# Edge attention of a graph network: both blocks of a pair in one operation, products written slot-innermost, one sum a pair

## The chip, the cores and the metric

One core of a Trainium2 chip (trn2). The metric is device time in microseconds (us) of one execution, lower is better. Engines: TensorE (PE), VectorE (DVE), ScalarE (ACT), GpSimd (POOL), SyncE (SP).

## What is computed

Two layers over 12500 nodes with 32 features and 200000 edges sorted by target. The first is a spline convolution (five gather and scatter stages that the change leaves alone). The second, which the change touches, is attention over each node's incoming edges with 4 heads, then a gated update:

```python
feat = (h @ W_gat).reshape(N, H, F)
e = leaky_relu(el[src] + er[dst], 0.2)
emax = segment_max(e, dst)
ee = exp(e - emax[dst])
alpha = ee / segment_sum(ee, dst)[dst]
agg = segment_sum(feat[src] * alpha[:, :, None], dst)
gi = agg.reshape(N, H * F) @ W_ih.T + b_ih
gh = h @ W_hh.T + b_hh
r, z = sigmoid(i_r + h_r), sigmoid(i_z + h_z)
n = tanh(i_n + r * h_n)
out = x + elu((1 - z) * n + z * h)
```

Since the sum over edges is linear, the kernel sums weight times `h[src]` (32 numbers a head, 4 x 32 = 128 a node) and applies `W_gat` and `W_ih` afterwards as one matrix.

## The kernel before

The change lies in `attention_flow` alone, the last stage. Nodes lie 128 to a block (one a partition), 98 blocks, worked in 49 pairs. Each node's edges are contiguous rows of the table `rows4` in HBM, 36 numbers an edge (32 features and 4 scores); one pass takes up to 40 edges of every node (RUN = 40), and here one pass is enough.

**POOL** (L1605 to L1660) runs two things in turn. `gather_turn` issues 32 indirect gathers (L1614), each of which fetches 128 rows of 36 numbers from the node table into a ring of four slots; SP writes a full slot out to `rows4` (L1586) and loads the next indices (L1564). `load_runs` (L1618) waits for those writes, then until both products of the pair before are made (`prod_made`, L1624), since `run` has one buffer a block of the pair, then issues two indirect loads (L1629), one for each block, of 40 x 36 numbers a partition. After a lead of two turns, every pair of blocks has its turn of gathers ahead of its run load until the gathers are through: there are 32 gathers between the run loads of pairs 0 to 46, and none behind that of pair 46.

**VectorE** (L1786 to L1812) does for each pair: `scale` of the pair before (L1695: divide the sums by the denominators), `attend` (L1790: copy of the next start rows for POOL at L1793, then `body` for block 0 and for block 1), and `gate` of the pair before (L1712). `body` (L1734) is a chain in which each step waits for the one ahead: mask of missing edges (L1742), score (L1744, L1746), leaky relu (L1748), maximum over edges (L1750, L1752), differences (L1754, L1756), the new maximum to `top` (L1758), the sum of the weights (L1760) once ScalarE has made the exponential (L1820), the denominator (L1766, L1771), the old sum times its factor as a 41st product (L1767), four products of 10 edges each (L1774), and their sum (L1783). The products of one block are 41 x 4 x 32, the edge ("slot") outermost, so that the sum over slots reads elements 128 words apart:

```python
dve.tensor_reduce(sums[:, v, :], prod[:, v, :, :, :].rearrange("p s h f -> p (h f) s"), X, ALU.add)
```

**ScalarE** (L1814 to L1854) makes the exponentials (`weigh`), copies for TensorE (`lift`), the sigmoid, tanh and exponential of the gates (`open_gates`), and copies each block's sums into the accumulator (`take`, L1822), which `scale` waits for (`added`, L1697). **TensorE** (L1856) transposes and multiplies for the gates.

Nothing orders the engines but these semaphores: each engine's instructions run in the order written. Outside the attention stage the text uses only the durations of single lines: L139 and L298 (sums over contiguous elements), L207 (a dense cast), L213 (a copy to every eighth word) and L761 (an operation with two inputs whose elements lie five words apart in all operands).

Of the kernel before, what the change touches and what calls it, by code (L numbers as in the profile page):

```python
# [29 lines left out]
FEAT = 32  # L30
HID = 64
K = 125
HEADS = 4
BIG = 1e30
# [6 lines left out]
SLOPE = 0.2  # L41
# [3 lines left out]
GW = FEAT + HEADS  # L45
RUN = 40
# [13 lines left out]
def bc(ap, shape):  # L60
    return ap.to_broadcast(shape)
# [1448 lines left out]
def attention_flow(nc, c, d, sem, out):  # L1510
# [6 lines left out]
    prod_made, summed, added = (sem(f"at_{x}") for x in ("prod_made", "summed", "added"))  # L1517
# [7 lines left out]
    steps, gate_steps = 13, 7  # L1525
    H3 = 3 * FEAT
    HALF = NB // 2
    full = (N // P) * P
    with nc.Block() as block, ExitStack() as ctx:
        sb, ps, _ = allocators(nc, ctx)  # L1530
# [8 lines left out]
        out_of = sb("at_out_of", [P, 2, RUN])  # L1539
        score = sb("at_score", [P, 2, RUN, HEADS])  # L1540
        peak, total = sb("at_peak", [P, 2, HEADS]), sb("at_total", [P, 2, HEADS])
        weight = sb("at_weight", [P, 2, RUN + 1, HEADS])
        prod = sb("at_prod", [P, 2, RUN + 1, HEADS, FEAT])
        sums = sb("at_sums", [P, 2, P])
# [118 lines left out]
        def _(dve):  # L1663
# [10 lines left out]
            dve.sem_inc(summed, 2)  # L1674
# [20 lines left out]
            def scale(i, item):  # L1695
                pair = bass.ds(i * 2, 2)
                dve.wait_ge(added, item * 2 + (NB + 2))  # L1697
                dve.wait_ge(turned, item + 1)
                dve.tensor_copy(hs[:, :, :], c.h[:, pair, :]).then_inc(gate_seq, 1)
                dve.tensor_scalar(rden[:, :, :], c.acc[:, pair, P:P + HEADS], 1e-30, None, ALU.max).then_inc(gate_seq, 1)  # L1700
                dve.wait_ge(gate_seq, item * gate_steps + 2)
                dve.reciprocal(rden[:, :, :], rden[:, :, :]).then_inc(gate_seq, 1)
                dve.wait_ge(gate_seq, item * gate_steps + 3)
                for v in range(2):
                    last = dve.tensor_tensor(xs[:, v, :, :],
                                             c.acc[:, bass.ds(i * 2 + v, 1), 0:P].rearrange("p b (h f) -> p (b h) f", h=HEADS),
                                             bc(rden[:, v, :].unsqueeze(2), [P, HEADS, FEAT]), ALU.mult)
                    if v == 0:
                        last.then_inc(gate_seq, 1)
                last.then_inc(scaled, 1)  # L1710

            def gate(i, item):  # L1712
# [4 lines left out]
                dve.wait_ge(gate_seq, item * gate_steps + 5)  # L1717
                dve.tensor_tensor(cand[:, :, :], g_ps[:, :, 2 * FEAT:H3], gap[:, :, :], ALU.add).then_inc(shaped, 1)
                dve.wait_ge(curved, item + 1)
                dve.tensor_tensor(gap[:, :, :], c.h[:, pair, :], cand[:, :, :], ALU.subtract).then_inc(gate_seq, 1)  # L1720
                dve.wait_ge(gate_seq, item * gate_steps + 6)
                dve.tensor_tensor(gap[:, :, :], gap[:, :, :], rz[:, :, FEAT:2 * FEAT], ALU.mult).then_inc(gate_seq, 1)
                dve.wait_ge(gate_seq, item * gate_steps + 7)
# [10 lines left out]
            def body(b, item, v):  # L1734
                def after_step(k):
                    dve.wait_ge(seq, item * steps + k)  # L1736

                el = run[:, v, :, FEAT:GW]
                er = bc(c.elr[:, bass.ds(b, 1), HEADS:2 * HEADS], [P, RUN, HEADS])
                best = top[:, bass.ds(b, 1), :].rearrange("p b h -> p (b h)")  # L1740
                s = score[:, v, :, :]
                dve.tensor_scalar(out_of[:, v, :], slots[:, :], left[:, bass.ds(b, 1)], -BIG, ALU.is_ge, ALU.mult)\  # L1742
                    .then_inc(seq, 1)
                dve.tensor_tensor(s, el, er, ALU.add).then_inc(seq, 1)  # L1744
                after_step(2)
                dve.tensor_tensor(s, s, bc(out_of[:, v, :].unsqueeze(2), [P, RUN, HEADS]), ALU.add).then_inc(seq, 1)  # L1746
                after_step(3)
                dve.scalar_tensor_tensor(s, s, SLOPE, s, ALU.mult, ALU.max).then_inc(seq, 1)  # L1748
                after_step(4)
                dve.tensor_reduce(peak[:, v, :], s.rearrange("p s h -> p h s"), X, ALU.max).then_inc(seq, 1)  # L1750
                after_step(5)
                dve.tensor_tensor(peak[:, v, :], peak[:, v, :], best, ALU.max).then_inc(seq, 1)  # L1752
                after_step(6)
                dve.tensor_tensor(weight[:, v, 0:RUN, :], s, bc(peak[:, v, :].unsqueeze(1), [P, RUN, HEADS]),  # L1754
                                  ALU.subtract).then_inc(exp_ready, 1)
                dve.tensor_tensor(weight[:, v, RUN, :], best, peak[:, v, :], ALU.subtract).then_inc(exp_ready, 1)  # L1756
                dve.wait_ge(exp_ready, item * 2 + 2)  # L1757
                dve.tensor_tensor(best, peak[:, v, :], peak[:, v, :], ALU.max).then_inc(seq, 1)  # L1758
                dve.wait_ge(exp_done, item + 1)  # L1759
                dve.tensor_reduce(total[:, v, :], weight[:, v, 0:RUN, :].rearrange("p s h -> p h s"), X, ALU.add)\  # L1760
                    .then_inc(seq, 1)

                dve.wait_ge(summed, item + 1)
                dve.wait_ge(added, item + 1)  # L1764
                den = c.acc[:, bass.ds(b, 1), P:P + HEADS].rearrange("p b h -> p (b h)")
                dve.tensor_tensor(den, den, weight[:, v, RUN, :], ALU.mult).then_inc(seq, 1)  # L1766
                dve.tensor_tensor(prod[:, v, RUN, :, :],  # L1767
                                  c.acc[:, bass.ds(b, 1), 0:P].rearrange("p b (h f) -> p (b h) f", h=HEADS),
                                  bc(weight[:, v, RUN, :].unsqueeze(2), [P, HEADS, FEAT]), ALU.mult)
# [12 lines left out]
                dve.wait_ge(added, item + (NB - 1))  # L1782
                dve.tensor_reduce(sums[:, v, :], prod[:, v, :, :, :].rearrange("p s h f -> p (h f) s"), X, ALU.add)\  # L1783
                    .then_inc(summed, 1)

            n = dve.value_load(c.run_passes[0:1, 0:1], min_val=1, max_val=EP // RUN + 1)  # L1786
            with dve.Fori(0, n) as o:
                dve.wait_ge(pass_begun, o + 1)
                dve.sem_inc(dve_turn, 1)
                def attend(i):  # L1790
                    for v in range(2):
                        dve.wait_ge(run_loaded[v], i * 16 + 16)  # L1792
                    dve.tensor_copy(run_at[:, :], runs[:, bass.ds(i * 2 + 2, 2)]).then_inc(run_at_made, 1)  # L1793
                    for v in range(2):
                        body(i * 2 + v, o * NB + i * 2 + v, v)
# [3 lines left out]
                attend(0)  # L1799
                with dve.Fori(1, HALF) as i:  # L1800
                    scale(i - 1, o * HALF + i - 1)
                    attend(i)
                    gate(i - 1, o * HALF + i - 1)
# [11 lines left out]
        def _(act):  # L1815
            act.sem_inc(added, NB)
# [24 lines left out]
            with act.Fori(0, n) as o:  # L1841
                for v in range(2):
                    weigh(o * NB + v, v)
                for v in range(2):
                    take(v, o * NB + v, v)
                with act.Fori(1, HALF) as i:
                    lift(o * HALF + i - 1)
                    for v in range(2):
                        weigh(o * NB + i * 2 + v, v)
                    open_gates(o * HALF + i - 1)  # L1850
                    for v in range(2):
                        take(i * 2 + v, o * NB + i * 2 + v, v)
                lift(o * HALF + HALF - 1)
                open_gates(o * HALF + HALF - 1)  # L1854
# [137 lines left out]
```

## Time and profile before

| | |
|---|---|
| median of 3 runs | 11170.6 us (11164.8 to 11173.6) |
| profiled execution, its span from first to last instruction | 12528.6 us |
| the profiled execution's own time, beside its span | none is given but the span |
| attention stage in it | about 9790 us to the end |
| VectorE busy | 62% |
| POOL busy | 60% |
| TensorE busy | 52% |
| ScalarE busy | 23% |

The profiled execution is longer than the timed ones by 1358 us. Register and branch instructions aren't counted as busy. The busy shares are means over stages with different limits, and a row of one stage has to be read against the time of that stage.

### The profile page before, as it was taken

The numbers are of one execution on the slowest core, as the hardware profiler recorded it, in microseconds if no ns is written. First come the engines' busy times: TensorE is split into PE (matmuls) and PEld (weight loads), VectorE is DVE, ScalarE is ACT, GpSimd is POOL, SyncE is SP. The second block draws the span as 40 slices with busy tenths as digits, with TensorE's granted clock in tenths as the row PEclk, the third lists the DMA queues.
The fourth block names the chain that finished last, engine by engine and source line by source line (L and its number), as shares of the span: only waits on it lengthen the run. The fifth ranks groups of instructions, "written<-read, shape, count | busy, mean of one in ns | idle before, by whom it ended". The sixth has DMA issues, their size and how long they took to land. (4 is left out here: it accounts for less than half of the span.)

```text
span 12528.6 us, 178083 instructions
## 1 busy us (share of the span) xinstructions
PE 6505.4 (52%) x38968; PEld 5397.9 (43%) x38968; DVE 7716.2 (62%) x17239; ACT 2933.1 (23%) x8407; POOL 7476.5 (60%) x7456
## 2 busy tenths in 40 slices
PE   3466666666475799999994444545555100000000
PEld 2355555555475677777764434434454100000000
DVE  9844444444498676666664444544576267777777
ACT  0011111111132344344432222322343000000001
POOL 5155555655200888888886888888800566666663
PEclk9966666666698999999997667766777555555555
DMA  1210000000733444444443333333322212221221
GB/s 41 65 36 2 2 2 2 2 2 2 14 41 50 93 93 94 92 94 95 92 93 49 50 51 53 54 50 52 54 42 34 35 49 50 51 50 48 51 54 40
DMA packets 1788557, 605.09 MB, mean 48 GB/s; under 512 B 1595943, under 2 KB 1729575, under 8 KB 1788260
## 3 DMA queue, kind: packets, MB, share of 16 engines
q1 hardware_dynamic: 1078132, 311.05, 12.8%
q0 software_dynamic: 255648, 274.30, 10.7%
q10 hardware_dynamic: 454736, 19.28, 3.0%
q8 instruction: 15, 0.25, 0.0%
q14 instruction: 26, 0.21, 0.0%
HBM read 430.75 MB, written 172.95 MB: 48 GB/s over the span
## 5 line engine op out<-in xcount | busy, mean ns | idle before, releaser
L1222 PE MATMUL c_acc<-c_spread_sb,c_basis_sb 128*125 128x256 f32 (+1 forms) x12544 | 2599.2, 376 | 1502.8 <-issue 655.0
L1222 PEld LDWEIGHTS c_acc<-c_spread_sb,c_basis_sb 128*125 128x125 f32 x12544 | 2266.5, 231 | 1803.5 <-issue 1536.3
L1614 POOL DMA_INDIRECT at_ring<-gat_table,at_place x1568 | 1585.7, 1011 | 1188.5 <-issue 1188.5
L609 POOL DMA_INDIRECT rec<-rk_rec,rk_place x1568 | 1619.3, 1033 | 1110.1 <-DVE rk_place L497 620.7
L1321 ACT ACTIVATE c_sums<-c_acc 125x512 f32<-125x512 f32 (+1 forms) x3136 | 1489.3, 490 | 2258.7 <-PE c_acc L1222 1298.6
L961 POOL DMA_INDIRECT c_ring<-hid_table,c_at x1568 | 1707.1, 1089 | 478.9 <-issue 443.2
L961 POOL DMA_INDIRECT c_ring<-feat_table,c_at x1568 | 1602.7, 1022 | 478.1 <-issue 462.9
L1084 DVE TENSOR_TENSOR c_spread_sb<-c_mark,c_rin 128x512 f32<-128x512 f32 (+1 forms) x3136 | 1745.2, 557 | 60.3
L1871 PE MATMUL gr_hps<-ident,gr_hs 128*32 128x128 f32 x98 | 29.8, 408 | 2473.7 <-issue 2066.3
L492 DVE CUSTOM_DVE_ANT_0 rk_junk_l<-rk_look_ps,rk_hi 128x98 bf16<-128x98 f32 x1568 | 402.2, 257 | 1324.1 <-remote 821.1
L1234 PE MATMUL c_mix<-c_sums,c_w 125*64 125x256 f32 (+1 forms) x9408 | 1037.3, 401 | 187.6 <-issue 133.8
L554 PE MATMUL rk_look_ps<-rk_table,rk_lo_t 128*128 128x98 f32 x3136 | 908.7, 425 | 379.5 <-DVE rk_before L492 327.4
L1871 PEld LDWEIGHTS gr_hps<-ident,gr_hs 128*32 128x32 f32 x98 | 6.4, 109 | 2488.1 <-issue 2078.1
L554 PEld LDWEIGHTS rk_look_ps<-rk_table,rk_lo_t 128*128 128x128 f32 x3136 | 705.4, 292 | 503.3 <-DVE rk_before L492 404.2
L1783 DVE TENSOR_REDUCE at_sums<-at_prod 128x128 f32<-128x5248 f32 x98 | 873.3, 8911 | 24.0 <-issue 14.1
L1234 PEld LDWEIGHTS c_mix<-c_sums,c_w 125*64 125x64 f32 (+1 forms) x9408 | 627.4, 132 | 559.2 <-issue 304.0
L530 PE MATMUL rk_rows_ps<-ident,rk_cols 128*128 128x128 f32 x3152 | 771.1, 390 | 4.7 <-ACT rk_cols L564 4.5
L1110 DVE TENSOR_SCALAR c_rel<-c_rin,first 128x16 f32<-128x16 f32 x392 | 103.3, 264 | 1014.6 <-DMA c_rin<-rows 434.9
L587 ACT ACTIVATE rk_table<-rk_run_ps 128x98 f32<-128x98 f32 x784 | 196.2, 250 | 2173.9 <-PE rk_run_ps L549 1208.1
L530 PEld LDWEIGHTS rk_rows_ps<-ident,rk_cols 128*128 128x128 f32 x3152 | 664.9, 292 | 6.4 <-ACT rk_cols L564 6.4
L1144 DVE SCALAR_TENSOR_TENSOR c_hat<-c_hat,c_sides 128x96 f32<-128x96 f32 x196 | 52.5, 268 | 985.3 <-issue 785.6
L487 DVE SCALAR_TENSOR_TENSOR rk_junk<-rk_rows_ps,src_f,rk_earlier 128x128 bf16<-128x128 f32 (+1 forms) x1568 | 647.2, 413 | 2.0 <-PE rk_rows_ps L530 2.0
(356 smaller groups left out, 10126.9 us busy)
## 6 DMA issues: line engine op xcount, KB each, us to landing
c_rin<-rows SPq DMA_DIRECT2D x3136, 42.0 KB
c_rin<-rows SPq DMA_DIRECT2D x3136, 20.0 KB
rows<-c_ring POOLq DMA_DIRECT2D x392, 128.0 KB
rows<-rk_blank SPq DMA_DIRECT2D x112, 252.0 KB
rows<-c_ring POOLq DMA_DIRECT2D x392, 72.0 KB
rows<-at_ring SPq DMA_DIRECT2D x196, 144.0 KB
rec<-rk_rec,rk_place POOLq DMA_INDIRECT x1568
c_ring<-hid_table,c_at POOLq DMA_INDIRECT x1568
```

The lines of the kernel that those rows point to most:

```text
L487: dve.scalar_tensor_tensor(junk[:, u, j // 2, odd:2 * odd + 1, :], rows[:, u, j - odd:j + 1, :], c.src[:, bass.ds(g * G + j, 1)], earlier[ ...
L492: dve.tensor_tensor_reduce(junk_l[:, u, j, :], look[:, j % 2, 0:NB], hi_hot[:, u, j, :], 1.0, 0.0, ALU.mult, ALU.add, before[:, u, j:j + 1 ...
L530: last = pe.matmul(rows[:, u, j, :], bc(cols[:, u, j:j + 1], [P, P]), c.ident[:, :], start=True, stop=True)
L554: pe.matmul(look[:, j % 2, 0:NB], lo_t[:, u, j, :], table[:, k % 2, :], start=True, stop=True).then_inc(looked, 1)
L609: pool.indirect_dma_start(out=d.rec, out_offset=bass.IndirectOffsetOnAxis(ap=place[:, u, j:j + 1], axis=0), in_=rec[:, u, j, :], in_offset ...
L961: pool.indirect_dma_start(out=ring[:, u, j, :], out_offset=None, in_=table, in_offset=bass.IndirectOffsetOnAxis(ap=at[:, h, u, j:j + 1], a ...
L1084: dve.tensor_tensor(spread[:, q, w, :, :], bc(mark[:, q, w, :].unsqueeze(2), [P, 2, feats, WN]), bc(rin[:, q, w, 0:feats].unsqueeze(3), [P ...
L1222: last = pe.matmul(acc[pp % BANKS][:, (w % 2) * WN * feats:(w % 2 + 1) * WN * feats], basis[:, q, w, :, :].rearrange("p a b -> p (a b)"), ...
L1234: last = pe.matmul(mix[k * outs:(k + 1) * outs, 0:2 * P], wsb[:, f, :], sums[:, f, :], start=(i_f == 0), stop=(i_f == each - 1))
L1321: act.activation(sums[:, :, at:at + 2 * WN].rearrange("p f (k n) -> p k f n", n=WN), acc[pp % BANKS][:, 0:pair].rearrange("p (k f n) -> p ...
L1614: pool.indirect_dma_start(out=ring[:, u, j, :], out_offset=None, in_=d.gat_table, in_offset=bass.IndirectOffsetOnAxis(ap=place[:, u, j:j + ...
L1783: dve.tensor_reduce(sums[:, v, :], prod[:, v, :, :, :].rearrange("p s h f -> p (h f) s"), X, ALU.add)\
```

## The change

Each small step handles both blocks of a pair in one operation. `out_of` and `score` are laid out so that both blocks are one run of 80 slots, the mask keeps 0 or 1 and its multiplication by -BIG moves into the operation that adds it. `prod` is laid out with the slot innermost (41 words from one head-feature to the next), the four products a block write it in steps of 41 words, and one sum a pair reads it contiguously and writes into the accumulator, so that `sums`, the semaphore `added` and ScalarE's copies go. The store to `top` moves behind the products. The two operations of `scale` that divide become one. POOL, SP and TensorE are unchanged; `prod_made` is still counted once a block.

The diff of `attention_flow`, with renumbered waits, declarations and the loop's plain rewriting left out:

```diff
-        out_of = sb("at_out_of", [P, 2, RUN])
-        score = sb("at_score", [P, 2, RUN, HEADS])
+        out_of = sb("at_out_of", [P, 2 * RUN])
+        score = sb("at_score", [P, 2 * RUN, HEADS])
         peak, total = sb("at_peak", [P, 2, HEADS]), sb("at_total", [P, 2, HEADS])
         weight = sb("at_weight", [P, 2, RUN + 1, HEADS])
-        prod = sb("at_prod", [P, 2, RUN + 1, HEADS, FEAT])
-        sums = sb("at_sums", [P, 2, P])
+        prod = sb("at_prod", [P, 2, HEADS * FEAT, RUN + 1])
...
-                dve.wait_ge(added, item * 2 + (NB + 2))
+                dve.wait_ge(summed, item + 2)
...
-                for v in range(2):
-                    last = dve.tensor_tensor(xs[:, v, :, :],
-                                             c.acc[:, bass.ds(i * 2 + v, 1), 0:P].rearrange("p b (h f) -> p (b h) f", h=HEADS),
-                                             bc(rden[:, v, :].unsqueeze(2), [P, HEADS, FEAT]), ALU.mult)
-                    if v == 0:
-                        last.then_inc(gate_seq, 1)
-                last.then_inc(scaled, 1)
+                dve.tensor_tensor(xs[:, :, :, :], c.acc[:, pair, 0:P].rearrange("p b (h f) -> p b h f", h=HEADS),
+                                  bc(rden[:, :, :].unsqueeze(3), [P, 2, HEADS, FEAT]), ALU.mult).then_inc(scaled, 1)
...
-            def body(b, item, v):
+            def attend(i, item):
+                pair = bass.ds(i * 2, 2)
+                real, rest = weight[:, :, 0:RUN, :], weight[:, :, RUN, :]
+
                 def after_step(k):
                     dve.wait_ge(seq, item * steps + k)
 
-                el = run[:, v, :, FEAT:GW]
-                er = bc(c.elr[:, bass.ds(b, 1), HEADS:2 * HEADS], [P, RUN, HEADS])
-                best = top[:, bass.ds(b, 1), :].rearrange("p b h -> p (b h)")
-                s = score[:, v, :, :]
-                dve.tensor_scalar(out_of[:, v, :], slots[:, :], left[:, bass.ds(b, 1)], -BIG, ALU.is_ge, ALU.mult)\
+                for v in range(2):
+                    dve.wait_ge(run_loaded[v], i * 16 + 16)
+                dve.tensor_copy(run_at[:, :], runs[:, bass.ds(i * 2 + 2, 2)]).then_inc(run_at_made, 1)
+                dve.tensor_tensor(out_of[:, :].rearrange("p (v s) -> p v s", v=2), bc(slots[:, :].unsqueeze(1), [P, 2, RUN]),
+                                  bc(left[:, pair].unsqueeze(2), [P, 2, RUN]), ALU.is_ge).then_inc(seq, 1)
+                dve.tensor_tensor(score[:, :, :].rearrange("p (v s) h -> p v s h", v=2), run[:, :, :, FEAT:GW],
+                                  bc(c.elr[:, pair, HEADS:2 * HEADS].unsqueeze(2), [P, 2, RUN, HEADS]), ALU.add)\
                     .then_inc(seq, 1)
-                dve.tensor_tensor(s, el, er, ALU.add).then_inc(seq, 1)
                 after_step(2)
-                dve.tensor_tensor(s, s, bc(out_of[:, v, :].unsqueeze(2), [P, RUN, HEADS]), ALU.add).then_inc(seq, 1)
+                dve.scalar_tensor_tensor(score[:, :, :], bc(out_of[:, :].unsqueeze(2), [P, 2 * RUN, HEADS]), -BIG,
+                                         score[:, :, :], ALU.mult, ALU.add).then_inc(seq, 1)
                 after_step(3)
-                dve.scalar_tensor_tensor(s, s, SLOPE, s, ALU.mult, ALU.max).then_inc(seq, 1)
+                dve.scalar_tensor_tensor(score[:, :, :], score[:, :, :], SLOPE, score[:, :, :], ALU.mult, ALU.max)\
+                    .then_inc(seq, 1)
                 after_step(4)
-                dve.tensor_reduce(peak[:, v, :], s.rearrange("p s h -> p h s"), X, ALU.max).then_inc(seq, 1)
+                dve.tensor_reduce(peak[:, :, :], score[:, :, :].rearrange("p (v s) h -> p v h s", v=2), X, ALU.max)\
+                    .then_inc(seq, 1)
                 after_step(5)
-                dve.tensor_tensor(peak[:, v, :], peak[:, v, :], best, ALU.max).then_inc(seq, 1)
+                dve.tensor_tensor(peak[:, :, :], peak[:, :, :], top[:, pair, :], ALU.max).then_inc(seq, 1)
                 after_step(6)
-                dve.tensor_tensor(weight[:, v, 0:RUN, :], s, bc(peak[:, v, :].unsqueeze(1), [P, RUN, HEADS]),
-                                  ALU.subtract).then_inc(exp_ready, 1)
-                dve.tensor_tensor(weight[:, v, RUN, :], best, peak[:, v, :], ALU.subtract).then_inc(exp_ready, 1)
-                dve.wait_ge(exp_ready, item * 2 + 2)
-                dve.tensor_tensor(best, peak[:, v, :], peak[:, v, :], ALU.max).then_inc(seq, 1)
+                dve.tensor_tensor(real, score[:, :, :].rearrange("p (v s) h -> p v s h", v=2),
+                                  bc(peak[:, :, :].unsqueeze(2), [P, 2, RUN, HEADS]), ALU.subtract).then_inc(exp_ready, 1)
+                dve.tensor_tensor(rest, top[:, pair, :], peak[:, :, :], ALU.subtract).then_inc(exp_ready, 1)
                 dve.wait_ge(exp_done, item + 1)
-                dve.tensor_reduce(total[:, v, :], weight[:, v, 0:RUN, :].rearrange("p s h -> p h s"), X, ALU.add)\
-                    .then_inc(seq, 1)
+                dve.tensor_reduce(total[:, :, :], real.rearrange("p v s h -> p v h s"), X, ALU.add).then_inc(seq, 1)
 
                 dve.wait_ge(summed, item + 1)
-                dve.wait_ge(added, item + 1)
-                den = c.acc[:, bass.ds(b, 1), P:P + HEADS].rearrange("p b h -> p (b h)")
-                dve.tensor_tensor(den, den, weight[:, v, RUN, :], ALU.mult).then_inc(seq, 1)
-                dve.tensor_tensor(prod[:, v, RUN, :, :],
-                                  c.acc[:, bass.ds(b, 1), 0:P].rearrange("p b (h f) -> p (b h) f", h=HEADS),
-                                  bc(weight[:, v, RUN, :].unsqueeze(2), [P, HEADS, FEAT]), ALU.mult)
-                after_step(9)
-                dve.tensor_tensor(den, den, total[:, v, :], ALU.add).then_inc(seq, 1)
-                for k in range(4):
-                    w = slice(k * RUN // 4, (k + 1) * RUN // 4)
-                    last = dve.tensor_tensor(prod[:, v, w, :, :],
-                                             bc(weight[:, v, w, :].unsqueeze(3), [P, RUN // 4, HEADS, FEAT]),
-                                             bc(run[:, v, w, 0:FEAT].unsqueeze(2), [P, RUN // 4, HEADS, FEAT]), ALU.mult)
-                    if k < 3:
-                        last.then_inc(seq, 1)
-                        after_step(11 + k)
-                last.then_inc(prod_made, 1)
-                dve.wait_ge(prod_made, item + 3)
-                dve.wait_ge(added, item + (NB - 1))
-                dve.tensor_reduce(sums[:, v, :], prod[:, v, :, :, :].rearrange("p s h f -> p (h f) s"), X, ALU.add)\
-                    .then_inc(summed, 1)
+                den = c.acc[:, pair, P:P + HEADS]
+                dve.tensor_tensor(den, den, rest, ALU.mult).then_inc(seq, 1)
+                dve.tensor_tensor(prod[:, :, :, RUN].rearrange("p v (h f) -> p v h f", h=HEADS),
+                                  c.acc[:, pair, 0:P].rearrange("p b (h f) -> p b h f", h=HEADS),
+                                  bc(rest.unsqueeze(3), [P, 2, HEADS, FEAT]), ALU.mult)
+                after_step(8)
+                dve.tensor_tensor(den, den, total[:, :, :], ALU.add).then_inc(seq, 1)
+                for v in range(2):
+                    for k in range(4):
+                        w = slice(k * RUN // 4, (k + 1) * RUN // 4)
+                        last = dve.tensor_tensor(prod[:, v, :, w].rearrange("p (h f) s -> p s h f", h=HEADS),
+                                                 bc(weight[:, v, w, :].unsqueeze(3), [P, RUN // 4, HEADS, FEAT]),
+                                                 bc(run[:, v, w, 0:FEAT].unsqueeze(2), [P, RUN // 4, HEADS, FEAT]), ALU.mult)
+                        if k < 3:
+                            last.then_inc(seq, 1)
+                            after_step(10 + v * 3 + k)
+                    last.then_inc(prod_made, 1)
+                    dve.wait_ge(prod_made, item * 2 + v + 3)
+                dve.tensor_tensor(top[:, pair, :], peak[:, :, :], peak[:, :, :], ALU.max).then_inc(seq, 1)
+                dve.tensor_reduce(c.acc[:, pair, 0:P], prod[:, :, :, :], X, ALU.add).then_inc(summed, 1)
...
-            def weigh(item, v):
+            def weigh(item):
                 act.wait_ge(exp_ready, item * 2 + 2)
-                act.activation(weight[:, v, :, :], weight[:, v, :, :], ACT.Exp).then_inc(exp_done, 1)
-
-            def take(b, item, v):
-                act.wait_ge(summed, item + 3)
-                act.activation(c.acc[:, bass.ds(b, 1), 0:P].rearrange("p b f -> p (b f)"), sums[:, v, :], ACT.Copy)\
-                    .then_inc(added, 1)
```

## Rows read from the trace of the kernel before

**Rows 1.** The page: its head, and busy us (share) xinstructions of each engine.
```profile
span 12528.6 us, 178083 instructions
PE 6505.4 (52%) x38968; PEld 5397.9 (43%) x38968; DVE 7716.2 (62%) x17239; ACT 2933.1 (23%) x8407; POOL 7476.5 (60%) x7456
```
**Rows 2.** Groups of instructions of the attention stage.
```profile
L1783 DVE TENSOR_REDUCE at_sums<-at_prod 128x128 f32<-128x5248 f32 x98 | 873.3, 8911 | 24.0 <-issue 14.1 <-DVE at_prod L1774 0.2
L1774 DVE TENSOR_TENSOR at_prod<-at_weight,at_run 128x1280 f32<-128x1280 f32 x392 | 583.9, 1489 | 19.7 <-remote 7.2 <-DVE at_prod L1774 1.6 <-issue 1.1
L1760 DVE TENSOR_REDUCE at_total<-at_weight 128x4 f32<-128x160 f32 x98 | 42.4, 432 | 62.4 <-issue 57.2 <-ACT at_weight L1820 5.2
L1614 POOL DMA_INDIRECT at_ring<-gat_table,at_place x1568 | 1585.7, 1011 | 1188.5 <-issue 1188.5
```
**Rows 3.** Timeline of VectorE, one pair without gathers: start us, us, instruction.
```profile
12382.79 0.17 DVE L1793 COPY at_run_at<-at_runs 128x2 uint32 x1
12382.92 0.24 DVE L1742 TENSOR_SCALAR at_out_of<-at_slots,at_left 128x40 f32<-128x40 f32 x1
...
12386.41 6.05 DVE L1774 TENSOR_TENSOR at_prod<-at_weight,at_run 128x1280 f32<-128x1280 f32 x4
12392.59 8.91 DVE L1783 TENSOR_REDUCE at_sums<-at_prod 128x128 f32<-128x5248 f32 x1
12401.42 0.23 DVE L1742 TENSOR_SCALAR at_out_of<-at_slots,at_left 128x40 f32<-128x40 f32 x1
...
12423.18 0.20 DVE L1699 COPY gr_hs<-h 128x64 f32 x1 [0.61 <-ACT acc L1824]
...
12424.33 0.17 DVE L1793 COPY at_run_at<-at_runs 128x2 uint32 x1
```
**Rows 4.** Timeline of POOL: run loads of pairs 0, 37, 38 and 46.
```profile
9921.71 0.95 POOL L1629 DMA_INDIRECT at_run<-rows,at_run_at  x1 [0.30 <-issue]
...
11898.14 0.94 POOL L1629 DMA_INDIRECT at_run<-rows,at_run_at  x1 [8.30 <-issue]
...
11944.96 0.95 POOL L1629 DMA_INDIRECT at_run<-rows,at_run_at  x1 [0.31 <-issue]
...
12370.47 0.94 POOL L1629 DMA_INDIRECT at_run<-rows,at_run_at  x1 [10.40 <-issue]
```
**Rows 5.** Timeline of POOL and VectorE: gathers while one block's products are made.
```profile
11918.03 6.06 DVE L1774 TENSOR_TENSOR at_prod<-at_weight,at_run 128x1280 f32<-128x1280 f32 x4
11918.21 2.12 POOL L1614 DMA_INDIRECT at_ring<-gat_table,at_place  x1 [0.31 <-issue]
11920.64 1.22 POOL L1614 DMA_INDIRECT at_ring<-gat_table,at_place  x1 [0.30 <-issue]
11922.16 1.22 POOL L1614 DMA_INDIRECT at_ring<-gat_table,at_place  x1 [0.30 <-issue]
...
11925.21 0.95 POOL L1614 DMA_INDIRECT at_ring<-gat_table,at_place  x1 [0.30 <-issue]
```
**Rows 6.** Groups of VectorE elsewhere: contiguous sums, dense and strided writes.
```profile
L139 DVE TENSOR_REDUCE ln_stat<-ln_tmp 128x98 f32<-128x3136 f32 x1 | 3.4, 3420 | 0.0
L298 DVE TENSOR_REDUCE cnt_lower<-cnt_below 128x7 f32<-128x784 f32 x14 | 13.6, 970 | 0.5
L207 DVE CAST src_f<-src_i 128x1568 f32<-128x1568 int32 x1 | 1.0, 976 | 0.0
L213 DVE COPY rec_sb<-src_f 128x1568 f32<-128x1568 f32 x1 | 1.6, 1575 | 0.0
L761 DVE SCALAR_TENSOR_TENSOR c_keep<-c_keep,c_sides 128x54 f32<-128x54 f32 x196 | 40.0, 249 | 87.7 <-ACT c_keep L668 87.7
```
**Rows 7.** Chain of work, 12267 to 12275 us: DVEq is VectorE's sequencer.
```profile
12267.49 0.05 DVEq L1705
...
12269.05 0.71 DVEq L1792
...
12271.17 0.73 DVEq L1792
```

More of the change, by code:

```diff
@@ L1516, in attention_flow @@
                                                                           "exp_done"))
-    prod_made, summed, added = (sem(f"at_{x}") for x in ("prod_made", "summed", "added"))
+    prod_made, summed = sem("at_prod_made"), sem("at_summed")
     pass_begun, stores_issued, dve_turn = (sem(f"at_{x}") for x in ("pass_begun", "stores_issued", "dve_turn"))
@@ L1524, in attention_flow @@
                                  "updated", "gate_seq", "out_stored"))
-    steps, gate_steps = 13, 7
+    steps, gate_steps = 16, 6
     H3 = 3 * FEAT
@@ L1673, in _ @@
             dve.sem_inc(prod_made, 2)
-            dve.sem_inc(summed, 2)
+            dve.sem_inc(summed, 1)
             dve.sem_inc(updated, 1)
@@ L1716, in gate @@
                 dve.tensor_tensor(gap[:, :, :], g_ps[:, :, H3:P], rz[:, :, 0:FEAT], ALU.mult).then_inc(gate_seq, 1)
-                dve.wait_ge(gate_seq, item * gate_steps + 5)
+                dve.wait_ge(gate_seq, item * gate_steps + 4)
                 dve.tensor_tensor(cand[:, :, :], g_ps[:, :, 2 * FEAT:H3], gap[:, :, :], ALU.add).then_inc(shaped, 1)
@@ L1720, in gate @@
                 dve.tensor_tensor(gap[:, :, :], c.h[:, pair, :], cand[:, :, :], ALU.subtract).then_inc(gate_seq, 1)
+                dve.wait_ge(gate_seq, item * gate_steps + 5)
+                dve.tensor_tensor(gap[:, :, :], gap[:, :, :], rz[:, :, FEAT:2 * FEAT], ALU.mult).then_inc(gate_seq, 1)
                 dve.wait_ge(gate_seq, item * gate_steps + 6)
-                dve.tensor_tensor(gap[:, :, :], gap[:, :, :], rz[:, :, FEAT:2 * FEAT], ALU.mult).then_inc(gate_seq, 1)
-                dve.wait_ge(gate_seq, item * gate_steps + 7)
                 dve.tensor_tensor(cand[:, :, :], cand[:, :, :], gap[:, :, :], ALU.add).then_inc(least, 1)
@@ L1789, in _ @@
                 dve.sem_inc(dve_turn, 1)
[L1790 to L1795, printed above, removed]
                 dve.wait_ge(runs_ready, o + 1)
                 dve.tensor_copy(run_at[:, :], runs[:, 0:2]).then_inc(run_at_made, 1)
-                attend(0)
+                attend(0, o * HALF)
                 with dve.Fori(1, HALF) as i:
                     scale(i - 1, o * HALF + i - 1)
-                    attend(i)
+                    attend(i, o * HALF + i)
                     gate(i - 1, o * HALF + i - 1)
@@ L1815, in _ @@
         def _(act):
-            act.sem_inc(added, NB)
-            def weigh(item, v):
+            def weigh(item):
                 act.wait_ge(exp_ready, item * 2 + 2)
-                act.activation(weight[:, v, :, :], weight[:, v, :, :], ACT.Exp).then_inc(exp_done, 1)
-            def take(b, item, v):
-                act.wait_ge(summed, item + 3)
-                act.activation(c.acc[:, bass.ds(b, 1), 0:P].rearrange("p b f -> p (b f)"), sums[:, v, :], ACT.Copy)\
-                    .then_inc(added, 1)
+                act.activation(weight[:, :, :, :], weight[:, :, :, :], ACT.Exp).then_inc(exp_done, 1)
             def lift(item):
@@ L1841, in _ @@
             with act.Fori(0, n) as o:
[L1842 to L1845, printed above, removed]
+                weigh(o * HALF)
                 with act.Fori(1, HALF) as i:
                     lift(o * HALF + i - 1)
-                    for v in range(2):
-                        weigh(o * NB + i * 2 + v, v)
+                    weigh(o * HALF + i)
                     open_gates(o * HALF + i - 1)
-                    for v in range(2):
-                        take(i * 2 + v, o * NB + i * 2 + v, v)
                 lift(o * HALF + HALF - 1)
```

## The prediction, made before the changed kernel was run

> **What bounds the kernel now.** I read the page first, for the share of each engine [rows 1], then the groups of the attention stage, the only one that the change touches [rows 2], then the timeline of VectorE in a pair of blocks, then that of POOL. No engine is busy throughout: VectorE and POOL work in turns through `run`, which has one buffer for a pair. POOL issues two run loads as soon as the eight products of the pair before are made, then 32 gathers for later blocks, then waits for products again.
>
> VectorE's own pace is seen at the end of the stage, where no gathers are left: from the copy of `run_at` of one pair to that of the next 12424.33 - 12382.79 = 41.5 us [rows 3]. In it the small steps of one block take 12386.41 - 12382.92 = 3.5 us, its four products 6.05, its sum 8.9, twice; gate and scale fill the rest. POOL's own pace is seen in the pair in which it waited for nothing: from one run load to the same of the next pair 11944.96 - 11898.14 = 46.8 us. The 46 pairs with gathers take (12370.47 - 9921.71) / 46 = 53.2 us each on average [rows 4].
>
> Why 46.8? 34 transfers, one every 1.25 us, are 42.6 us. Under VectorE's products they come one per product: the gather issued at 11918.21, just after the first product began, takes 2.12 us, and the next ones start 1.52 apart, VectorE's pace, and take 1.22; under the sum the time is 0.95 again, and the start-to-start time 1.25 [rows 5, 2]. So 26 x 1.25 + 8 x 1.53 + 2 x 0.9 (the first gather of each group of four, 2.12 against 1.22) = 46.5, which is the 46.8 of the row. A gather waits at its start for the end of whatever product runs, and gets one chance per product.
>
> Why 53.2 and not 46.8? In stretches VectorE's register instructions take 0.7 us instead of 0.05 [rows 7], and the small steps of a block grow with them. The profiled execution spans 12528.6 us [rows 1], 1358 us above the median of 11170.6 us. I can't see from one trace whether those stretches exist without the profiler. I take it as likelier that they don't: a sixth of the gap would be theirs, 46 x (53.2 - 46.8) = 294 us. So two readings stand: (a) in the timed runs POOL sets 46.8 us a pair; (b) 53.2 us there too. Differences are worked out against the trace and then put on the median.
>
> **The parts.**
>
> One sum a pair. The two sums read elements 128 words apart: 8.91 us for 5248, (8911 - 153) / 5248 = 1.67 ns each. Sums over contiguous elements cost 970 ns for 784 and 3420 for 3136: 1.042 ns each and 153 ns fixed [rows 6]. The new one reads 2 x 5248 of them: 10496 x 1.042 + 153 = 11.1 us instead of 17.8, -6.7 us a pair.
>
> Products written slot-innermost. Their reads stay, but each element now goes 41 words behind the last. Now 1489 ns for 1280 elements, 1.04 ns each [rows 2]. No row writes 41 words apart. The nearest: a copy to every eighth word takes 1575 ns where a dense one of the same count takes 976; both write two elements a step, 784 steps, so a step is 1.81 ns against 1.05. And L761, a two-input operation whose elements lie five words apart, costs (249 - 153) / 54 = 1.78 ns [rows 6]. I take 1.81: 1280 x 1.81 + 153 = 2.47 us, 2.5 with the gap; eight are 19.8 instead of 12.2 us, +7.6. Lower end: nothing, if 0.91 ns per written element (1.81 for two) is the store's limit, under the 1.04 at which products run. Upper end: a step that suits the memory worse costs twice the extra, 1.04 + 2 x 0.77 = 2.58 ns, 3.45 us a product. Below nothing is excluded: the operation can't be shorter than its elements at 1.04.
>
> Small steps of both blocks in one operation. Doubled elements add 4 x 0.17 (additions and subtractions over 160 elements), 2 x 0.28 (the two reductions, 432 ns for 160 elements 4 words apart [rows 2]), 0.15 each for the exponential and the accumulator's product, 0.04 for the mask, and 256 x 0.77 ns = 0.2 for that product's own writes 41 words apart: 1.8. One chain of 3.5 + 1.8 = 5.3 replaces two of 3.5: -1.7. The store to `top`, hidden now by ScalarE's exponential, moves ahead of the sum: +0.2. The in-place sum drops ScalarE's copy, for which scale waits 0.61 us [rows 3], and one of two operations in scale: -0.6. Together -2.1. Waits on `added` go; nothing was queued behind them for long. ScalarE, TensorE and SP are idle most of the stage and get no new wait.
>
> So VectorE's pair is 41.5 - 6.7 + 7.6 - 2.1 = 40.3 us. That alone would be worth 1.2 us a pair.
>
> POOL. Its instructions stay, and `prod_made` is reached as before. But the chances now come every 2.5 us: eight gathers go by in 19.8 us, 26 transfers outside take 32.6, and one group instead of two costs one first wait, some 0.6: 53.0 us a pair against 46.8. All products lie under gathers: at the latest VectorE starts 12.3 us after the run load (12370.47 to 12382.79), products from 17.6 to 37.4, and gathers go on to 53. VectorE's slack of 13 us covers its own longer tail after the products (11.1 of sum for 8.9). So 46 x 6.2 = +285 us, the last three pairs, with no gathers, 3 x -1.2: +281.
>
> The Trainium skill, "SBUF — State Buffer", section "Who interferes with whom", says that an operation of VectorE with two inputs in SBUF contends with a GpSimd instruction that reads SBUF, and that the first keeps the port for the whole instruction. By that rule a gather waits for whole products, and the trace agrees (2.12 us for 0.95).
>
> **Forecast:** 11170.6 + 281 = about 11450 us, from reading (a), 2.5 us a product and one gather per product. Chance 0.36; its own range is 11380 to 11520.
>
> **Rivals.**
> - The slow register stretches are in the timed runs as well, (b). For: they are in the trace, 53.2 a pair. Against: the gap to the median. VectorE's small steps, once instead of twice, lose less to them; a slow chain of some 18 us instead of 5, after a tail of 15, and 19.8 of products end 53 us after the run load, together with POOL; with the hand-over 54.5 instead of 53.2. +60: 11230 us. Chance 0.18.
> - The 41-word step is dearer, up to 3.45 us a product. For: no row has this step. Against: steps of 4, 5, 8 and 128 words all show 1.67 to 1.81 ns. POOL: 32.6 + 8 x 3.48 + 0.6 = 61.0 us a pair, 46 x 14.2 + 3 x 6.5 = +673: 11840 us; half-way values as likely. Chance 0.2.
> - Faster: strided writes are free for an operation that writes one element a step (the lower end). Against: L761. Then products stay at 1.49, VectorE's pair falls to 41.5 - 6.7 - 2.3 = 32.5, and POOL's to 46.8 - 0.9 since one first wait goes: 46 x 0.9 + 3 x 9.0 = 68 us less, 11100 us; in reading (b) some 250 less. It decides below about 1.55 us a product. With all other ways to get there, 0.17.
> - POOL isn't held to one gather per long product (it waits only for part of one), so that 46.8 stands; or the two effects cancel. No change, 11165 us. Chance 0.09. The skill gives a ground in the same section: it takes the write interface to be what issuing a transfer needs, and such an operation to hold the read interface alone (it calls this inferred); by that no product would hold a gather, against the 2.12 us.
>
> The Trainium skill, "Vector Engine (DVE) Microarchitecture Reference", section "5.2 Measured stream behaviour on trn2", gives 1.71 ns for a destination that hops 4 KiB every element and 2.50 to 2.51 for one that steps 24 words. An estimate from the second is 1280 x 2.5 + 153 = 3.35 us a product, near my upper end; no row here shows a 24-word step.
>
> **Numbers.** The likeliest case gives 11450. The range 11170 to 11760 holds it, (b), the unchanged case and the lower half of the dear writes; outside are nearly all of the faster cases and the dearest writes. About 0.2% (22 us) is what a measurement can tell from no change. Faster by more 0.17, within 0.1 (unchanged, and a small part of b), slower 0.73.
>
> **What would show it.** The product's group at 2.4 to 2.5 us x392 and the new sum at 11.1 x49; gathers under products 2.5 us apart; run loads 53 us apart, with POOL never waiting for products. Products at 1.5 us, or gathers 1.25 apart under long products, would prove it wrong. The profile's own span should grow less than the timed runs, by some 60 us, if the slow stretches belong to the profiler.

## The result and the profile after

The changed kernel is slower, as forecast: median 11469.7 us (4 runs) against 11172.1 us, ratio 1.0269 with a 95% interval of 1.0257 to 1.0282. The forecast was 11450 us, range 11170 to 11760. The kernel before now has four timed runs; the three that the forecast used have a median of 11170.6 us. Here the profiled execution agrees with the timed ones (span 11472.3 us), so its rows can be set against the median directly.

The groups of the attention stage, which answer to [rows 2] (busy us, mean ns of one, idle time ahead):

```profile
L1772 DVE TENSOR_TENSOR at_prod<-at_weight,at_run 128x1280 f32<-128x1280 f32 x392 | 953.6, 2433 | 11.8
L1781 DVE TENSOR_REDUCE acc<-at_prod 128x10496 f32 x48 | 531.8, 11079 | 0.0
L1759 DVE TENSOR_REDUCE at_total<-at_weight 128x8 f32<-128x320 f32 x49 | 35.0, 715 | 26.6 <-ACT at_weight L1808 26.6
L1613 POOL DMA_INDIRECT at_ring<-gat_table,at_place x1568 | 1955.6, 1247 | 701.8 <-issue 701.5 <-DMA rows<-at_ring 0.3
```

The product went from 1489 to 2433 ns; one sum of 11.08 us replaces two of 8.91. VectorE's busy time over the whole kernel fell from 7716.2 to 7663.8 us, since small steps shrank too. But the mean gather, an instruction that the change doesn't touch, went from 1011 to 1247 ns. (The second profile of the kernel before, e1 below, has 7694.9 us and 1059 ns.) Why is in the timeline of POOL and VectorE under one pair's products, which answers to [rows 5], and of the next run load:

```profile
10490.24 1.07 POOL L1613 DMA_INDIRECT at_ring<-gat_table,at_place  x1 [0.30 <-issue]
10491.61 0.94 POOL L1613 DMA_INDIRECT at_ring<-gat_table,at_place  x1 [0.30 <-issue]
...
10492.33 19.69 DVE L1772 TENSOR_TENSOR at_prod<-at_weight,at_run 128x1280 f32<-128x1280 f32 x8
10492.86 2.59 POOL L1613 DMA_INDIRECT at_ring<-gat_table,at_place  x1 [0.30 <-issue]
10495.75 2.17 POOL L1613 DMA_INDIRECT at_ring<-gat_table,at_place  x1 [0.30 <-issue]
10498.22 2.16 POOL L1613 DMA_INDIRECT at_ring<-gat_table,at_place  x1 [0.30 <-issue]
10500.69 2.16 POOL L1613 DMA_INDIRECT at_ring<-gat_table,at_place  x1 [0.30 <-issue]
10503.15 2.17 POOL L1613 DMA_INDIRECT at_ring<-gat_table,at_place  x1 [0.30 <-issue]
...
10531.79 0.94 POOL L1628 DMA_INDIRECT at_run<-rows,at_run_at  x1 [0.30 <-issue]
```

Gathers start 2.47 us apart while products run, one for each, and 1.25 apart outside. A gather that comes late like this, and the delay itself, is called held and the hold below. Nothing but POOL's own 0.30 us lies ahead of the run load: as long as there are gathers (run loads of pairs 0 to 46), POOL never waits for VectorE. VectorE waits for POOL instead, some 15 us a pair; the source view of the run loads has, for L1628:

```profile
who waited for it (us, times):
  DVE at_run_at L1737: 695.8, 47
```

The run loads of pairs 0 and 46 [rows 4] are now at

```profile
8894.14 0.94 POOL L1628 DMA_INDIRECT at_run<-rows,at_run_at  x1 [0.30 <-issue]
...
11322.41 0.94 POOL L1628 DMA_INDIRECT at_run<-rows,at_run_at  x1 [0.30 <-issue]
```

so a pair takes (11322.41 - 8894.14) / 46 = 52.8 us.

### The profile page after: what moved, and what is told of

The parts are those of the page before. It is cut to its first block and busy times, and to the rows that moved or that the text cites. A ratio compares the mean times of both kernels' runs of the same rounds, so it can differ in the third digit from the quotient of the medians.

```text
span 11472.3 us, 175984 instructions
## 1 busy us (share of the span) xinstructions
PE 5924.7 (52%) x38968; PEld 5064.6 (44%) x38968; DVE 7663.8 (67%) x16504; ACT 2978.8 (26%) x8260; POOL 7897.7 (69%) x7456
## 5 line engine op out<-in xcount | busy, mean ns | idle before, releaser
L1613 POOL DMA_INDIRECT at_ring<-gat_table,at_place x1568 | 1955.6, 1247 | 701.8 <-issue 701.5
L1772 DVE TENSOR_TENSOR at_prod<-at_weight,at_run 128x1280 f32<-128x1280 f32 x392 | 953.6, 2433 | 11.8
L1234 PE MATMUL c_mix<-c_sums,c_w 125*64 125x256 f32 (+1 forms) x9408 | 867.0, 380 | 24.6 <-ACT c_sums L1321 24.6
L554 PE MATMUL rk_look_ps<-rk_table,rk_lo_t 128*128 128x98 f32 x3136 | 700.8, 357 | 3.6 <-DVE rk_before L492 3.4
L1234 PEld LDWEIGHTS c_mix<-c_sums,c_w 125*64 125x64 f32 (+1 forms) x9408 | 543.4, 128 | 313.3 <-ACT c_sums L1321 34.7
L956 POOL COPY c_at<-dst_at 128x16 uint32 (+1 forms) x196 | 65.2, 333 | 859.2 <-POOLq L1907 858.5
L530 PE MATMUL rk_rows_ps<-ident,rk_cols 128*128 128x128 f32 x3152 | 656.7, 343 | 0.0
L549 PE MATMUL rk_run_ps<-rk_hi,rk_lo 128*128 128x98 bf16 x1568 | 238.2, 242 | 788.0 <-ACT rk_table L587 788.0
L968 POOL DMA_DIRECT2D rows<-c_ring x784 | 626.4, 799 | 14.1 <-DMA c_ring<-hid_table,c_at 8.6
L554 PEld LDWEIGHTS rk_look_ps<-rk_table,rk_lo_t 128*128 128x128 f32 x3136 | 574.9, 252 | 13.2 <-DVE rk_before L492 4.0
```

The costliest lines, as they stand in the source:

```text
L530: last = pe.matmul(rows[:, u, j, :], bc(cols[:, u, j:j + 1], [P, P]), c.ident[:, :], start=True, stop=True)
L554: pe.matmul(look[:, j % 2, 0:NB], lo_t[:, u, j, :], table[:, k % 2, :], start=True, stop=True).then_inc(looked, 1)
L968: pool.dma_start(rows_v[:, bass.ds(t * tiles + u * slot, slot), :], ring[:, u, :, :]).then_inc(stored[u], 16)
L1234: last = pe.matmul(mix[k * outs:(k + 1) * outs, 0:2 * P], wsb[:, f, :], sums[:, f, :], start=(i_f == 0), stop=(i_f == each - 1))
L1613: pool.indirect_dma_start(out=ring[:, u, j, :], out_offset=None, in_=d.gat_table, in_offset=bass.IndirectOffsetOnAxis(ap=place[:, u, j:j + ...
L1772: last = dve.tensor_tensor(prod[:, v, :, w].rearrange("p (h f) s -> p s h f", h=HEADS), bc(weight[:, v, w, :].unsqueeze(3), [P, RUN // 4, ...
```

## The experiments

Each experiment is compared with the kernel before, timed beside it on the same chip: 11198 us beside e1 to e4, 11180 beside e5 to e8 and 11188 (median of 7) beside e9 and e10. e1 to e8 were timed once each, and the kernel before alone moves between 11165 and 11198 us, so for small differences the time of a pair in the trace is the firmer number. "Apart" is always from start to start. "Own pair" is VectorE's time for a pair at the end of the stage, where no gathers are left.

**e1: the kernel before, once more.** No edit. The profile of the prediction was 1358 us longer than the timed runs, and the forecast hung on how that was read.

> The kernel before, unchanged, profiled once more. Theory (reading a of the prediction): the slow stretches of VectorE's register instructions belong to that one profiled execution; here run loads are 46.8 us apart in the 46 pairs with gathers, POOL never waits long for products, register instructions take 0.05 us, and the span is near 11170 us. Rival (reading b): the stretches are a part of the kernel; run loads are 50 to 53 us apart and some hundreds of register instructions take 0.7 us.

Measured: 11191.7 us, span 11189.9. Run loads of two neighbouring pairs, and the first lines of VectorE's groups:

```profile
10295.20 0.94 POOL L1629 DMA_INDIRECT at_run<-rows,at_run_at  x1 [0.30 <-issue]
...
10341.01 0.94 POOL L1629 DMA_INDIRECT at_run<-rows,at_run_at  x1 [0.30 <-issue]
```

```profile
L1783 DVE TENSOR_REDUCE at_sums<-at_prod 128x128 f32<-128x5248 f32 x98 | 873.3, 8911 | 11.9
L1774 DVE TENSOR_TENSOR at_prod<-at_weight,at_run 128x1280 f32<-128x1280 f32 x392 | 583.8, 1489 | 10.1
```

And the source view of the run loads over the pairs with gathers (window 8900 to 11037 us) has:

```profile
L1629 POOL DMA_INDIRECT at_run<-rows,at_run_at x93: 939/944/952, 8902.9 to 11035.9; - x93
its engine sat idle before it (us, times) until:
  issue: 28.3, 93
```

The mean over 46 pairs is 46.4 us, from 45.3 to 47.0; no register instruction of VectorE in the stage takes more than 0.4 us. 28.3 us of idle time ahead of 93 run loads is 0.30 each, so in none of these pairs did POOL wait for products. Reading (a) holds: POOL set the pace before as well. The durations of the two large operations are those of the first profile to the nanosecond; what differed was the time between operations. The slow stretches are not the profiler's in general either, as I had thought likely; they came in that one execution. It also lost some 1020 us ahead of the attention stage (the first gather at 9801.5 us against 8782.9 here), and 320 in it.

**e2: the layout alone**, on the kernel before.

```diff
-        prod = sb("at_prod", [P, 2, RUN + 1, HEADS, FEAT])
+        prod = sb("at_prod", [P, 2, HEADS, FEAT, RUN + 1])
```

(and the operands that write and sum it, accordingly).

> The kernel before with one part of the change: products written slot-innermost and each block's sum read over contiguous slots; small steps, two sums and ScalarE's copies stay. Theory (a gather waits for the end of a running product, POOL sets the pace): products 2.43 us, sums 5.6, POOL's pair 26 x 1.25 + 8 x 2.47 and two first waits, 53.5 us; 11172 + 46 x 6.7, about 11480 us. Rival (VectorE's own pace sets the pair): 41.5 + 7.6 - 6.6 = 42.5 us instead of 41.5, about 11220 us.

Measured: 11499.3 us, 301 above the kernel before; 53.0 us a pair between run loads (0.5 under the theory's), own pair 42.5. The layout alone costs the whole of the loss, on POOL; by VectorE's own pair it would have cost 1.0 x 49 = 49 us.

```profile
L1774 DVE TENSOR_TENSOR at_prod<-at_weight,at_run 128x1280 f32<-128x1280 f32 x392 | 953.3, 2432 | 10.1
L1783 DVE TENSOR_REDUCE at_sums<-at_prod 128x128 f32<-128x5248 f32 x98 | 550.7, 5620 | 12.0
```

**e3: everything but the layout.** The changed kernel with dense products again.

```diff
-        prod = sb("at_prod", [P, 2, HEADS * FEAT, RUN + 1])
+        prod = sb("at_prod", [P, 2, RUN + 1, HEADS * FEAT])
...
-                dve.tensor_reduce(c.acc[:, pair, 0:P], prod[:, :, :, :], X, ALU.add).then_inc(summed, 1)
+                dve.tensor_reduce(c.acc[:, pair, 0:P], prod[:, :, :, :].rearrange("p v s x -> p v x s"), X, ALU.add).then_inc(summed, 1)
```

(and the operands that write it, accordingly).

> The changed kernel with prod laid out slot-outermost again, so that products write densely and the one sum a pair reads 128 words apart: the other part of the change alone. Theory (POOL's pace with the hold): products 1.49 us, the sum 10496 x 1.669 + 153 ns = 17.7, VectorE's own pair 39.0, POOL's 46.8 less one first wait of 0.9: 45.9; about 11172 - 41 - 8 = 11120 us. Rival (VectorE sets the pair): 2.5 us a pair, about 11050 us.

Measured: 11144.0 us, 54 below the kernel before; 45.3 us a pair, own pair 39.1. Both numbers of VectorE and the sign are as the theory has them. 1.1 us a pair and the last pairs are all that 2.4 us less of VectorE's work bring. The two parts don't add up: beside the new layout the same small steps and single sum are worth only 0.2 us a pair (53.0 in e2, 52.8 in the changed kernel).

**e4: take away the second SBUF input.** The changed kernel, strided writes kept; ScalarE writes the exponentials to PSUM, and the products read them there.

```diff
-                act.activation(weight[:, :, :, :], weight[:, :, :, :], ACT.Exp).then_inc(exp_done, 1)
+                act.activation(expd, weight[:, :, :, :], ACT.Exp).then_inc(exp_done, 1)
...
-                                                 bc(weight[:, v, w, :].unsqueeze(3), [P, RUN // 4, HEADS, FEAT]),
+                                                 bc(expd[:, v, w, :].unsqueeze(3), [P, RUN // 4, HEADS, FEAT]),
```

(and the smaller operations that read the exponentials, accordingly).

> The changed kernel with ScalarE writing the exponentials to PSUM, from where the products and the sum of the weights read them; all else stays, the strided writes too. Theory (a gather is held because a product reads two inputs from SBUF): products stay near 2.43 us, gathers under them come 1.25 us apart, POOL's pair is 34 x 1.25 = 42.6 and VectorE's about 40.5; about 11470 - 46 x 10 = 11010 us. Rival (long or strided-writing instructions of VectorE hold POOL whatever they read): gathers stay 2.47 apart, 52.8 us a pair, 11470 us.

Measured: 11014.5 us, 184 below the kernel before. The group of the products, and the timeline under them:

```profile
L1775 DVE TENSOR_TENSOR at_prod<-at_eps,at_run 128x1280 f32<-128x1280 f32 x392 | 951.7, 2428 | 11.8
```

```profile
10193.74 19.66 DVE L1775 TENSOR_TENSOR at_prod<-at_eps,at_run 128x1280 f32<-128x1280 f32 x8
10194.54 0.94 POOL L1615 DMA_INDIRECT at_ring<-gat_table,at_place  x1 [0.30 <-issue]
10195.79 0.94 POOL L1615 DMA_INDIRECT at_ring<-gat_table,at_place  x1 [0.31 <-issue]
10197.04 0.95 POOL L1615 DMA_INDIRECT at_ring<-gat_table,at_place  x1 [0.30 <-issue]
```

The products are as long as before the edit, and the gathers under them don't notice them: 0.94 us each, 1.25 apart. A pair takes 42.7 us, which is POOL's 34 x 1.25 and 0.2. So it is neither the length of the products nor their strided writes that holds a gather, but that both inputs lie in SBUF. The Trainium skill, "SBUF — State Buffer", section "Who interferes with whom", states this condition, and the trace agrees; its inference in the same section, that issuing a transfer needs only the port which such an operation leaves free, fails against the 2.16 us above.

**e5 and e6: the same products in other pieces.** The changed kernel with eight operations of 5 edges a block, or two of 20, for four of 10.

```diff
-                    for k in range(4):
-                        w = slice(k * RUN // 4, (k + 1) * RUN // 4)
+                    for k in range(8):
+                        w = slice(k * RUN // 8, (k + 1) * RUN // 8)
```

(and the shapes and waits, accordingly; 2 for 8 in e6).

> The changed kernel with each block's products in eight operations of 5 edges (640 elements) instead of four of 10; same bytes, same strided writes. Theory (a gather waits for the end of the product that runs, one gather per product): products 640 x 1.78 + 153 ns = 1.29 us, gathers under them 1.32 us apart, POOL's pair 16 x 1.32 + 18 x 1.25 + 0.6 = 44.2 us instead of 52.8, VectorE's own 41.7; about 11470 - 46 x 8.6 + 4 = 11080 us. Rival (the hold is a share of the time that products run, whatever their length): gathers still need 19.8 us for eight, 52.8 us a pair or more, 11480 us.

> The changed kernel with each block's products in two operations of 20 edges (2560 elements). Theory (one gather per product): products 4.71 us, gathers under them 4.74 apart, four a pair; POOL's pair 30 x 1.25 + 4 x 4.74 + 0.8 = 57.3 us instead of 52.8; about 11470 + 46 x 4.5 = 11680 us, although VectorE has less to do. Rival (the hold is a share of the time): no change, 11470 us.

Measured: e5 11094.7 us, 44.3 us a pair, products of 1296 ns, gathers under them 1.33 apart. So the changed kernel with shorter products is 85 us below the kernel before. e6 11660.0 us, 57.0 us a pair, products of 4705 ns:

```profile
10100.21 18.93 DVE L1772 TENSOR_TENSOR at_prod<-at_weight,at_run 128x2560 f32<-128x2560 f32 x4
10100.75 4.86 POOL L1613 DMA_INDIRECT at_ring<-gat_table,at_place  x1 [0.30 <-issue]
10105.91 4.43 POOL L1613 DMA_INDIRECT at_ring<-gat_table,at_place  x1 [0.30 <-issue]
10110.65 4.44 POOL L1613 DMA_INDIRECT at_ring<-gat_table,at_place  x1 [0.30 <-issue]
10115.40 4.43 POOL L1613 DMA_INDIRECT at_ring<-gat_table,at_place  x1 [0.31 <-issue]
10119.25 11.08 DVE L1781 TENSOR_REDUCE acc<-at_prod 128x10496 f32 x1
```

Four products, four gathers. With the same bytes and less busy time (922 us for e5's 1016) the longer pieces cost 565 us. A gather needs one moment between products, and the number of such moments is what counts.

**e7: pieces that are too short.** e3 with eight products a block.

> The kernel of e3_steps_only (dense products) with eight operations of 5 edges a block. Theory (a gather comes back 1.25 us after it was let through and then waits for the next end of a product): products 0.82 us, ends 0.85 apart, so gathers under them come 1.70 us apart, every second product, worse than 1.53 with the longer products; 8 x 1.70 + 26 x 1.25 + 0.4 = 46.5 us a pair instead of 45.3, about 60 us slower than e3_steps_only. Rival (shorter products always cost gathers less): gathers under them 1.25 to 1.35 apart, about 43.5 us a pair, some 80 us faster than e3_steps_only.

Measured: 11165.6 us, 46.12 us a pair, 0.85 more than e3's 45.27, which over 46 pairs is 39 us. By the timed runs it is 14 below the kernel before, where e3 was 54 below: the same 40 us, though that difference alone is little above the spread of single runs.

```profile
9964.18 13.69 DVE L1772 TENSOR_TENSOR at_prod<-at_weight,at_run 128x640 f32<-128x640 f32 x16
9965.31 1.35 POOL L1613 DMA_INDIRECT at_ring<-gat_table,at_place  x1 [0.30 <-issue]
9966.97 1.42 POOL L1613 DMA_INDIRECT at_ring<-gat_table,at_place  x1 [0.30 <-issue]
9968.69 1.42 POOL L1613 DMA_INDIRECT at_ring<-gat_table,at_place  x1 [0.30 <-issue]
9970.41 1.41 POOL L1613 DMA_INDIRECT at_ring<-gat_table,at_place  x1 [0.30 <-issue]
```

Products of 0.82 us end 0.86 apart (13.69 / 16), and gathers come 1.72 apart, every second end: a gather that is back after 1.25 us has just missed one. The time went the way that only the theory gives.

Counted over all 46 pairs with gathers (times are medians over the gathers that start while a product runs):

| | one product, us | products | gathers that start under them | from start to start, us |
|---|---|---|---|---|
| e6 | 4.71 | 184 | 184 | 4.74 |
| changed kernel | 2.43 | 368 | 368 | 2.47 |
| kernel before (e1), e3 | 1.49 | 368 | 368 | 1.53 |
| e5 | 1.30 | 736 | 736 | 1.33 |
| e7 | 0.82 | 736 | 368 | 1.72 |

**e8: another step for the writes.** The changed kernel with rows of `prod` of 48 words.

```diff
-        prod = sb("at_prod", [P, 2, HEADS * FEAT, RUN + 1])
+        prod = sb("at_prod", [P, 2, HEADS * FEAT, 48])
...
-                dve.tensor_reduce(c.acc[:, pair, 0:P], prod[:, :, :, :], X, ALU.add).then_inc(summed, 1)
+                dve.tensor_reduce(c.acc[:, pair, 0:P], prod[:, :, :, 0:RUN + 1], X, ALU.add).then_inc(summed, 1)
```

> The changed kernel with rows of prod padded from 41 to 48 words, so that products write 48 words apart; the sum skips the padding. Theory 1 (a strided write costs the same whatever the step): products 2.43 us, 11470 us. Theory 2 (the step matters; a page of the notes has 2.5 ns for steps of 24 words, a part of this step): products up to 1280 x 2.5 + 153 ns = 3.35 us, POOL's pair 26 x 1.25 + 8 x 3.38 + 0.8 = 60.4 us, about 11820 us.

Measured: 11443.9 us, 51.7 us a pair.

```profile
L1772 DVE TENSOR_TENSOR at_prod<-at_weight,at_run 128x1280 f32<-128x1280 f32 x392 | 904.3, 2307 | 11.9
```

(2307 - 153) / 1280 = 1.68 ns an element against (2433 - 153) / 1280 = 1.78 for 41 words; the 153 ns are those of the sums in [rows 6]. For 41 words e5 and e6 give the same without them: (4705 - 1296) / (2560 - 640) = 1.78. Neither theory is right to the letter: the step matters a little, and 48 words are cheaper. The dear case isn't seen. A step of 24 words itself wasn't tried, so what the Trainium skill ("Vector Engine (DVE) Microarchitecture Reference", section 5.2) says of it stays untested.

**e9 and e10: is there a kernel that beats both?** e9 is the kernel before with the exponentials in PSUM, e10 is e3 with them; the edit is that of e4.

> The kernel before with ScalarE's exponentials written to PSUM and read from there, nothing else. Theory (the second SBUF input of the products holds POOL, and POOL sets the pace): no gather is held, POOL's pair 34 x 1.25 = 42.6 us against VectorE's 41.5, so about 42.9 instead of 46.4: 46 x 3.5 = 160 us less, ratio to before about 0.986. Rival (PSUM only helped the kernel with long products): no change.

> The parts that the runs found good, together: small steps of a pair in one operation and one sum in place, products dense (slot-outermost), exponentials in PSUM. Theory: POOL's 34 x 1.25 = 42.6 us a pair hides VectorE's 39 altogether; 42.7 us a pair, the last pairs 39 us: the same as e4_exp_in_psum within some 5 us, ratio to before about 0.985. Rival (VectorE's path still counts beside POOL's): some 46 us below e4_exp_in_psum for the shorter VectorE pair.

Measured, 4 runs each: e9 11019.2 us, ratio to before 0.9846 (0.983 to 0.9863); e10 11013.5 us, 0.9847 (0.9831 to 0.9864). Run loads are 42.6 and 42.7 us apart. e4, e9 and e10 lie within 6 us of each other, although VectorE's own pair is 39.9, 41.3 and 38.9 us. With the hold gone POOL's 34 transfers set the pace, and what VectorE does in less than 42.6 us is free. The best of them are 1.5% faster than the kernel before and 4% faster than the changed one. The intervals don't tell e9 from e10.

## Why the prediction was right

By its own steps:

- *What bounds the kernel.* POOL, in reading (a). I forecast 46.8 us a pair before and 53.0 after; e1 shows 46.4, the profile after 52.8. The difference of 6.4 us is 294 us over 46 pairs, less 4 for the last pairs, some 290; the forecast was 281. The measured loss is 297.6, and the 7 us above 290 are within what single executions of one kernel differ by. The estimate for the pace before was 0.4 too high: it came from one pair, and e1's pairs lie between 45.3 and 47.0.
- *The sum.* 11.1 us forecast, 11.08 measured.
- *The product.* 1.81 ns an element forecast from the copy to every eighth word, 1.78 measured, which is to the hundredth what L761 had [rows 6]. That it is so close is in part luck. L761's destination and first input step five words, but its second input (`sides`, whose last dimension is 2) steps two, not five as said ahead of the prediction, and it both reads and writes with a step, where the product only writes with one. The eight products were put at 19.8 us without the gaps between them; 19.69 with the gaps was measured, so a product taken 0.04 us too long made up for them.
- *Small steps.* One chain of 5.3 us for two of 3.5: in the profile after it runs from 11410.80 (mask) to 11415.91 (first product), 5.1 us. VectorE's own pair was forecast at 40.3 and is 40.2.
- *The hold.* One gather for each product: shown by e4 (it takes two SBUF inputs), e6 (four for four) and e7 (every second end). What the prediction quotes of the Trainium skill ("SBUF — State Buffer", section "Who interferes with whom") on keeping the port for the whole instruction stands there beside VectorE's two-port modes; that two SBUF inputs do the same is what e6 shows, 4.43 us under products of 4.71. The first wait of a group was priced by one pair and too high for the new layout: the theory of e2 has two of them and 53.5 us a pair, and 53.0 was measured.
- *Which reading.* Right that the slow stretches don't belong to the timed runs, and its 294 us in this stage stands against some 320; but the ground was partly wrong: I took them for the profiler's, and said that the span would grow less than the timed runs. It shrank by 1056 us, since the profiled execution before was a disturbed one and the one after wasn't. The sign that I named for this could not have told it. And 294 of 1358 us is over a fifth of the gap, not a sixth; the rest lay ahead of this stage, where nothing had been looked at. The choice of (a) rested on the gap to the median alone, not on a row that told the readings apart; e1 does.

The parts other than the layout did save time alone: e3 shows them at -54 us. The loss is made by an engine that the change doesn't touch.

## What to carry to other kernels

When GpSimd issues transfers beside VectorE, look at the duration of its instructions under each kind of VectorE operation: here a product with two inputs in SBUF held a transfer's issue to its end, and moving one input to PSUM made the kernel before 1.5% faster. Cost a change of VectorE's operations by the number and spacing of their ends as well as by their sum. And set the span of a profile beside the timed runs before reading waits from it: in the disturbed one the durations of VectorE's operations were good; the gaps between them weren't, nor was TensorE's busy time (6505.4 us, against 5902.4 in e1).

## What was not expected

- The same products cost less in steps of 48 words (1.68 ns an element) than of 41 (1.78), both against 1.04 dense.
- In e7 halving the products made POOL slower: gathers 1.72 us apart under products of 0.82 us, 1.53 under those of 1.49 us, and 1.33 under strided ones of 1.30 us. Of the lengths tried the one just above the 1.25 us in which a gather comes back held POOL least.
- One profiled execution in which instructions of VectorE's sequencer (register, branch and semaphore ones) took 0.7 us in stretches: 843 of the 2891 from the first gather on, with hardly a mark in the durations of its operations (7716.2 us busy, 7694.9 in e1). None of the eleven other profiles has them. They are not the whole disturbance: none comes before 9970 us, yet by 3080 us the execution was already 528 us behind e1, and SyncE's sequencer has 1965 instructions of 0.6 to 0.8 us where the other profiles have 70 to 98. What made it stays open.
